# Two layers over eight samples on one core: plain float32 products in the first two stages of sample 0, a split moved to GpSimd, transposes in pairs, and a shorter distance between two stages

## The reference, cut to what matters

```
w1, w2 = W1[ids0], W2[ids0]                  # one pair for each of 8 samples
h   = relu(x @ w1 + b1)                      # 512 -> 128
a   = x + h @ w2 + b2                        # 128 -> 512
x1  = x + layernorm(a) * gamma + beta
out = x1 + x1 @ W[ids1] + b                  # 512 -> 512
```

## Time and profile before

| | us |
|---|---|
| median of 3 runs | 348.62 (347.25 to 349.91) |
| the profiled execution's own time | 349.46 |
| span of its trace | 347.7 |
| PE busy | 316.9 (91%) |
| DVE busy | 284.0 (82%) |
| ACT busy | 221.4 (64%) |
| POOL busy | 178.1 (51%) |

### The profile page before, as it was taken

How to read it: one execution, slowest core, us unless ns; L and a number is a source line. 1 busy time by engine, 2 the same in 40 slices (tenths; PEclk the granted TensorE clock), 3 DMA queues, 4 the chain that set the end, 5 groups by cost and what they waited for, 6 DMA issues and landing times.

```text
span 347.7 us, 4910 instructions
## 1 busy us (share of the span) xinstructions
PE 316.9 (91%) x1448; PEld 250.8 (72%) x1448; DVE 284.0 (82%) x707; ACT 221.4 (64%) x402; POOL 178.1 (51%) x140
## 2 busy tenths in 40 slices
PE   8674556999999999999999999999999999999996
PEld 8342334778788787878787878878787878877884
DVE  2597789789998999899998999899999999887410
ACT  3533665487667786677668766778667765766332
POOL 2395545367553846295646755384539580740000
PEclk9985585799999999999999999999999999999999
DMA  5997256256876567746965688646964661111222
GB/s 163 328 375 252 64 167 208 71 161 212 297 247 183 159 216 259 233 139 186 318 204 168 213 286 257 184 151 213 272 226 143 217 233 65 60 60 60 92 90 90
DMA packets 40894, 65.38 MB, mean 188 GB/s; under 512 B 6052, under 2 KB 10148, under 8 KB 40868
## 3 DMA queue, kind: packets, MB, share of 16 engines
q1 hardware_dynamic: 40720, 64.81, 57.8%
q10 hardware_dynamic: 148, 0.26, 0.2%
HBM read 48.29 MB, written 16.78 MB: 187 GB/s over the span
## 4 chain that ended last, share of the span: by engine, by line
DVE 49%; PE 25%; ACT 14%; issue 9%; DMA 2%; SPq 1%; ACTq 0%
PE out_ps L554 17%; DVE xT_lo L389 12%; DVE y L403 10%; DVE x1T_lo L454 9%; DVE turn_ps L447 5%; ACT xT_hi L284 5%; DVE stats L408 4%; PE turn_ps L600 3%; PE h_ps L554 3%; ACT hT L311 3%; DVE shift L438 2%; PE down_ps L554 2%; DVE rstd L432 2%; DMA xT<-x_cols 2%; ACT w_hi L302 2%
## 5 line engine op out<-in xcount | busy, mean ns | idle before, releaser
L329 ACT ACTIVATE y<-y,shift,rstd 128x512 f32<-128x512 f32 x64 | 52.2, 816 | 76.9 <-DVE shift L438 76.9
L554 PE MATMUL out_ps<-x1T_hi,w_hi 128*128 128x512 f32 x256 | 101.1, 395 | 0.0
L554 PE MATMUL out_ps<-x1T_lo,w_hi 128*128 128x512 f32 x256 | 100.4, 392 | 0.0
L554 PE MATMUL out_ps<-x1T_hi,w_lo 128*128 128x512 f32 x256 | 100.2, 391 | 0.0
L500 POOL TENSOR_TENSOR xrow<-xrow,b_rows 128x512 f32<-128x512 f32 x64 | 89.7, 1413 | 1.3 <-DMA b_rows<-b_all 1.3
L389 DVE TENSOR_TENSOR xT_lo<-xT,xT_hi 128x512 fp32r<-128x512 f32 x64 | 71.3, 1115 | 10.9 <-ACT xT_hi L284 10.9
L447 DVE SCALAR_TENSOR_TENSOR turn_ps<-turn_ps,gamma_beta,xT 128x512 f32<-128x512 f32 x64 | 47.6, 744 | 20.1 <-PE turn_ps L600 20.1
L505 POOL TENSOR_TENSOR hT_lo<-hT,hT_hi 128x512 fp32r<-128x512 f32 x14 | 18.1, 1294 | 76.6 <-ACT hT_hi L318 76.6
L554 PEld LDWEIGHTS out_ps<-x1T_lo,w_hi 128*128 128x128 f32 x256 | 48.3, 189 | 10.8
L554 PEld LDWEIGHTS out_ps<-x1T_hi,w_lo 128*128 128x128 f32 x256 | 48.4, 189 | 10.6
L554 PEld LDWEIGHTS out_ps<-x1T_hi,w_hi 128*128 128x128 f32 x256 | 48.4, 189 | 10.3
(11 more groups left out here) (37 smaller groups left out, 375.3 us busy)
## 6 DMA issues: line engine op xcount, KB each, us to landing
xrow<-x_rows SPq DMA_DIRECT2D x32, 512.0 KB, 6.0
out_cols<-out_sb SPq DMA_DIRECT2D x64, 256.0 KB, 4.0
xT<-x_cols SPq DMA_DIRECT2D x30, 512.0 KB, 4.8
w<-w_all SPq DMA_DIRECT2D x8, 1024.0 KB, 6.3
w<-w_all SPq DMA_DIRECT2D x16, 256.0 KB, 5.9
b_rows<-b_all SPq DMA_DIRECT2D x8, 256.0 KB, 5.4
xT<-x_cols SPq DMA_DIRECT2D x3, 256.0 KB, 5.0
xT<-x_cols ACTq DMA_DIRECT2D x1, 256.0 KB, 2.6
```

The source lines that it names most:

```text
L329: nc.scalar.activation(y[:, i % WR, :], y[:, i % WR, :], ACT.Identity, bias=shift[:, r], scale=rstd[:, r]).then_inc(norm_done, 1)
L554: mm = nc.tensor.matmul(out, lhsT, rhs, start=first and n == 0, stop=last and n == len(terms) - 1)
```

## The change

- In sample 0 (tiles 0 to 7) `up` multiplies w1 and xT, and `down` hT and w2, as float32, one product instead of three. Nothing of sample 0 is split for them: `x_hi`, `x_lo`, `h_high`, `h_low`, `w1_high`, `w1_low`, `w2_high`, `w2_low` start with tile 8, block 2 and sample 1.
- `x_lo` of tiles 8 to 63 is on POOL, first in its step; every `h_low` is on POOL.
- `turn` does two tiles in a step, at s mod 4 = 1 (tiles s-5 and s-4) and 2 (tiles s-4 and s-3), first in PE's step. `merge`, `x1_high` and `x1_low` follow in pairs in the same step. `turn` of an even tile waits for `x1_low` of the tile before it.
- `out` follows `down` by 7 tiles instead of 9, `finish` by 8 instead of 10.
- w1 and w2 have two buffers; the loads no longer wait for the sample before.
- `w_diagonal` and `w_low` of sample 0 come one step later (s = 2 and 3 to 6); those of the others keep their steps.
- The order within the steps of ACT and DVE changes; ACT's queue issues column tiles 0 to 2 ahead of the ids; SP issues w2(0) ahead of b1, and w1(1) ahead of rows 2-3.

```
-    TURN = -4
-    MERGE = -5
-    OUT = -9
-    FINISH = -10
+    OUT = -7
+    FINISH = -8
...
+    def w_part(s):
+
+        m, part = s // PER, s % PER - (3 if s // PER == 0 else 2)
+        return m, part if 0 <= m < SAMPLES and -1 <= part < KC else None
+
+    def turned(s):
+
+        first = {1: s - 5, 2: s - 4}.get(s % BLOCK, -1)
+        return (first, first + 1) if there(first) else ()
...
             load_w1(0)
-            for k in range(1, KC):
-                load_first_cols(k)
+            load_first_cols(3)
             load_cols(4)
+            load_w2(0)
             load_b1(0)
-            load_w2(0)
             load_rows(0)
             load_b2(0)
             load_cols(6)
+            load_w1(1)
             load_rows(2)
             load_cols(8)
-            load_w1(1)
             load_rows(4)
...
             def step(s):                       # ACT
+                for i in turned(s):
+                    x1_high(i)
                 if there(s + FINISH):
                     finish(s + FINISH)
-                if there(s + MERGE):
-                    x1_high(s + MERGE)
+                if (s + UP) % BLOCK == BLOCK - 1 and there(s + UP):
+                    relu((s + UP) // BLOCK)
+                if PER <= s + XHI < TILES:
+                    x_hi(s + XHI)
+                if (s + UP) % BLOCK == BLOCK - 1 and PER <= s + UP < TILES:
+                    h_high((s + UP) // BLOCK)
                 if there(s + NORM):
                     normalise(s + NORM)
...
             def step(s):                       # DVE
+                tiles = turned(s)
+                if tiles:
+                    for i in tiles:
+                        merge(i)
+                    if there(s + NORM):
+                        rstd_start(s + NORM)
+                        rstd_newton(s + NORM)
+                    if there(s + DOWN):
+                        add_rows(s + DOWN)
+                    if there(s + NORM):
+                        rstd_end(s + NORM)
+                    for i in tiles:
+                        x1_low(i)
...
+            def x_lo(i):                       # POOL
+                pool.wait_ge(xhi_done, i - PER + 1)
+                nc.gpsimd.tensor_tensor(xT_lo[:, i % KC, :], xT[:, i % XC, :],
+                                        xT_hi[:, i % KC, :].bitcast(f32), ALU.subtract).then_inc(xlo_done, 1)
...
+                if i < PER:                    # up
+                    terms = [(w1[:, 0, k], xT[:, i % XC, :])]
+                else:
+                    hi, lo = w1_hi[:, m % 2, k], w1_lo[:, m % 2, k]
+                    terms = [(hi, xT_hi[:, k]), (lo, xT_hi[:, k]), (hi, xT_lo[:, k])]
+                product(h_ps[blk % 2][:], terms, first=k == 0, last=k == KC - 1).then_inc(up_done, 1)
...
+                if i < PER:                    # down
+                    terms = [(hT[:, blk % 2, rows], w2[:, 0, :])]
...
-                if i >= 2:                     # turn
-                    pe.wait_ge(x1lo_done, i - 1)
+                if i >= 2 and i % 2 == 0:
+
+                    pe.wait_ge(x1lo_done, i)
```

More of the change, by code:

```diff
@@ L113, in cond_resid_kernel @@
         ids0_in, ids1_in = sem("ids0_in"), sem("ids1_in")
-        w1_in, w2_in, w_in = sem("w1_in"), sem("w2_in"), sem("w_in")
+        w_in = sem("w_in")
+        w1_in = [sem(f"w1_in{k}") for k in range(2)]
+        w2_in = [sem(f"w2_in{k}") for k in range(2)]
         b2_in = [sem(f"b2_in{k}") for k in range(2)]
@@ L363, in step @@
                     w1_high(m + 1)
-                if part == 4 and 0 <= m + 1 < SAMPLES:
+                if part == 4 and 1 <= m + 1 < SAMPLES:
                     w2_high(m + 1)
[L366 to L369, removed]
+                m, k = w_part(s)
+                if k is not None and k >= 0:
+                    w_high(m, k)
                 if there(s + DOWN):
                     standard(s + DOWN)
-            nc.scalar.dma_start(xT[:, 0, :], x_cols[0:P, 0:NB]).then_inc(first_cols_in[0], 16)
+            for k in range(KC - 1):
+                nc.scalar.dma_start(xT[:, k, :], x_cols[k * P:(k + 1) * P, 0:NB]).then_inc(first_cols_in[k], 16)
             nc.scalar.dma_start(ids0[:], l0_ids).then_inc(ids0_in, 16)
@@ L385, in _ @@
             nc.vector.memset(eps[:], EPS).then_inc(eps_done, 1)
[L387 to L395, removed]
             def add_rows(i):
@@ L530, in step @@
             def step(s):
-                if (s + UP) % BLOCK == BLOCK - 1 and DVE_H_SPLITS <= (s + UP) // BLOCK < BLOCKS:
-                    h_low((s + UP) // BLOCK)
+                if PER <= s + XLO < TILES:
+                    x_lo(s + XLO)
                 if there(s + BIAS_ROWS):
                     bias_rows(s + BIAS_ROWS)
+                if (s + UP) % BLOCK == BLOCK - 1 and PER <= s + UP < TILES:
+                    h_low((s + UP) // BLOCK)
                 m, part = s // PER, s % PER
@@ L537, in step @@
                     w1_low(m + 1)
-                if part == 4 and 0 <= m + 1 < SAMPLES:
+                if part == 4 and 1 <= m + 1 < SAMPLES:
                     w2_low(m + 1)
-                if part == 1 and 0 <= m < SAMPLES:
+                m, k = w_part(s)
+                if k == -1:
                     w_diagonal(m)
-                if 2 <= part < 2 + KC and 0 <= m < SAMPLES:
-                    w_low(m, part - 2)
+                elif k is not None:
+                    w_low(m, k)
             pool.wait_ge(ident_done, 1)
-            w1_low(0)
             for s in range(FIRST + 1, TILES):
@@ L620, in step @@
             def step(s):
+                for i in turned(s):
+                    turn(i)
                 if there(s + DOWN):
@@ L632, in _ @@
                 nc.tensor.matmul(turn_ps[0][:, :P], ident[:], ident[:], start=True, stop=True)
-            first_up()
+            for i in range(BLOCK):
+                up(i)
             for s in range(BLOCK - UP, TILES - OUT):
```

132 lines of the change are left out of this document (62 added, 70 removed).

## The result

The changed kernel takes 325.63 us (median of 4 runs, 325.11 to 326.23) against 349.08 for the kernel before (4 runs). The ratio is 0.9335 with a 95% interval of 0.9301 to 0.9369: faster by 6.6%. Forecast were 324 (316 to 337). The profiled execution took 325.84 us, with a span of 324.1.

What follows compares the result with a forecast made beforehand. It took a chain through all engines to bound the fill and PE, waiting mostly for x_lo, the steady state. Out at 43.8, clock 1.3, PE work 273.1, tail 1.0 and finish 3.2 give 322.4, plus 1.8 is 324.2; forecast 324, range 316 to 337.

Steps and rivals of the forecast that it cites:

- Fill: Stage before the first out: b2 at 14.4, POOL's 23 operations 28.8, waits 0.6; out at 43.8 us instead of 62.2.
- The b2 term: Start of the fill: b2 lands at 14.4 us, as column loads issued earlier bring it 1.5 forward; bounds 13.4, 15.9.
- Steady state: Middle of the kernel: PE needs 18.05 us per block, 36.1 per sample instead of 37.7, without waits for x_lo.
- the pair's wait for x1_low: On PE, at a block's second pair of turns: covered by 0.3 us in the middle; 1.0 put for the tail.
- x_lo to POOL at 1.25: POOL's operations take 1.25 us each once x_lo leaves DVE; bounds 1.24 to 1.72.
- Clock: Start of out: 1.3 us for the first half-speed matmuls; bounds 0 and 2.5.
- the sum: Whole kernel: 43.8 + 1.3 + 273.1 + 1.0 + 3.2 = 322.4 us; 1.8 around it gives 324.2; forecast 324.
- The distance: Steps from down to out: 9 before, listed in the chain that holds the fill; no size of its own given.
- So POOL is last, with 2 to 4 us to spare.: End of the fill: DVE's x1_low of tile 3 near 38 to 40, PE by 41, out at 43.8 behind POOL.
- The chain that I named as next: Fill, on DVE: steps of sample 0 plus merges and x1_low per pair, x1_low of tile 3 near 38 to 40.
- Rival 2: Fill: the loads hold it, as the same bytes are asked for sooner; out at 52, time 332 us; chance 0.15.
- What they remove is on the path: Fill: float32 products remove splits of x, W1, h, W2 before the first down; some 3 us more PE, hidden.

Runs made afterwards that it cites:

- the split on POOL: The changed kernel with sample 0 split into hi and lo like the others, all its lo parts on POOL: 331.87 us.
- the fillers: The changed kernel with eleven float32 matmuls of the identity (128 columns) added in PE's wait before the first out: 323.36 us.

## Why the prediction was right, point by point

- *Fill.* Forecast 43.8 for the first out, measured 44.00. By terms: b2 at 14.4, measured 14.57; 0.6 us of waits, measured 1.0; 23 operations at 1.25, measured 1.23. The b2 term was hit partly by luck: the two column loads were to bring it 1.5 us forward, and taking the order of loads back moved it by 0.7; the rest of the 1.3 us between before and after has no cause shown. That POOL is the last chain is shown by the run with three operations more (3.0 us for 3.0 us of work, and 0.26 for b2) and by the split on POOL (6.3 for six operations).
- *Steady state.* Forecast 36.1 us per sample without waits, measured 36.2 with PE at 40.00 of 40. The pair was put at 0.8 and costs 0.79; the pair's wait for x1_low stayed covered in the middle, as worked out, and in the tail PE's weight loads wait 1.1 us for x1_low, where 1.0 was put. That x_lo on DVE was what PE waited for is shown by the run with it back.
- *x_lo to POOL at 1.25.* The rows 1.24 and 1.72 of before were read rightly: with no large DVE operation of two SBUF inputs left, x_lo on POOL has a mean duration of 1.294 us and bias_rows 1.290, with 1.23 from start to start. The Trainium skill (SBUF — State Buffer, "Who interferes with whom") states that a DVE instruction with two SBUF inputs contends with a GpSimd instruction that reads SBUF. The runs agree where DVE got such an operation back: 1.70 us for x_lo and 1.31 for w_low there, and 1.7 us for the POOL operations that meet them.
- *Clock.* The term that was mis-sized: 1.3 us for the half-speed start of out, within bounds of 0 to 2.5. It measured 5.1-2.7 = 2.4, as nearly the whole first out runs at half clock; the fillers take 2.3 of it away. With it the sum would have been 325.3, against 325.84 of the profiled execution.
- *The distance.* I let it stand in the sum without a price of its own, and would have given it 2 to 3 us. Alone it is worth nothing: both distances lose 2.1 to 2.4 us to the half clock, and 0.4 us is what is left by my estimate.
- *"So POOL is last, with 2 to 4 us to spare."* The chain that I named as next is where I put it: x1_low of tiles 2 and 3 starts at 38.52 and takes 1.40 us, to 39.9 (forecast 38 to 40), 4.1 us before out. What I did not see is that the loads stand closer to POOL than that chain. More work on POOL costs in full, while the versions that moved work from POOL to DVE started out 0.4 us earlier at best: rows 6-7 land near 27.9, just when POOL comes to them, and w_low on DVE makes DVE's own chain the last. Work taken from POOL and put nowhere was not tried. Rival 2, the loads, is not what held this kernel, but it stands right behind POOL.
- *The float32 products.* "What they remove is on the path" holds for the lo parts on POOL only. The chain ahead of the first down, which I named as the reason, is not on the path: with the first down 3.3 us later, out came 0.9 us later, and POOL's rows account for that. A product of two records costs 0.86 us at full clock, as the records of the warm-ups gave it (0.9).
- *DVE and POOL.* I forecast 71 us less on DVE and 70 more on POOL; it was 284.0-228.6 = 55 and 236.8-178.1 = 59. For DVE I took the x_lo group's time, but the times of its groups overlap: before, they add up to 330 us and the engine was busy for 284; after, to 254 and 229. So a group's time is not what the engine gets back. For POOL, 56 x_lo at 1.294 us are 72.5, less 89.7-82.5 = 7.2 for bias_rows, which no longer meet x_lo, and 21.1-18.0 = 3.1 for two w_low fewer: 62 by the groups, and here too some of it is overlap. No step of the sum hung on either number.
- *The arithmetic of the sum.* 64 x 2.74 is 175.4 and 56 x 0.69 is 38.6, where it has 175.0 and 38.9; the total stays within 0.1 us.

The share of the parts, as far as the runs separate them (they are not additive): x_lo on POOL 17 us with the pairs in place, no lo parts of sample 0 on POOL 6, pairs 4 (measured at distance 9), loads at most 1, distance 0. The second buffers of w1 and w2 and the later `w_diagonal` were not taken back by themselves.

## What to carry to other kernels

Ask of each part of a change which of two limits it touches: here the fill was a queue of small operations on the slowest engine, and the middle was PE with an engine that came late. A chain that is last by a full engine can be lengthened at full price and still not be shortened, because a load or another engine stands right behind it; look in the timeline for what lands just before it is used. Before counting on work moved off it, ask what the engine that gets the work holds up. When a stage starts after a wait, look at the granted clock of its first big matmuls: fillers in the wait can be worth more than starting earlier.

## What the runs showed of the hardware that I had not expected

Eleven filler matmuls over 2.6 us, in a wait of 2.7 us, kept the granted clock full, and were worth 2.3 us. Six of them (1.5 us), with 1.4 us of idle time left before out, did as well: the first out then took from 44.09 to 46.98. So the gap didn't have to be covered in full. With x_lo back on DVE, the first out came after a wait of 1.4 us without any filler, and ran at full clock too. How little would do was not tried.

The half clock is easy to miss when two versions are compared by the start of one stage: at distance 9 it fell on the work ahead of out, at distance 7 on out itself, and cost about the same.
